# Edge passes of a graph kernel: from 2 gather buffers of 14 columns to 8 of 7, and the edge features and one table fill moved beside the second map scatter

## The chip, the cores and the metric

One NeuronCore of a Trainium2 chip runs the whole program. Its engines are TensorE (PE), VectorE (DVE), ScalarE (ACT), GpSimd (POOL) and the sync engine (SP), each with an instruction stream of its own; semaphores order them. The metric is the device time of one launch in microseconds, the median of three timed runs.

## The reference, cut to what matters

`x` holds 100,000 nodes of 96 float32 features, and `src`, `dst` name the ends of 50,000 edges. Four graph layers follow one another. All of them gather rows of a node table by edge and add them up by node:

```python
# layer 0: ten hops of a weighted sum over edges      layer 1: one GCN convolution
for _ in range(10):
    out = segment_sum(out[dst] * w[:, None], src, n) * 0.9 + h * 0.1
# layer 2: Chebyshev terms of degree 1, 2, 3 with softmax weights, then batch norm
Tx1 = prop(Tx0); Tx2 = 2.0 * prop(Tx1) - Tx0; Tx3 = 2.0 * prop(Tx2) - Tx1   # prop = weighted segment_sum(h[src], dst)
# layer 3: two GINE convolutions; e is computed once per edge
e = relu(edge_weight1 @ W_l0 + b_l0) @ W_l1 + b_l1          # [50000, 96]: the "edge features"
agg = segment_sum(relu(x[src] + e), dst, n)
# after each layer: x = layernorm(x + layer(x))
```

## The kernel before, in words

The edges are sorted twice, by `src` (`sort_src`) and by `dst` (`sort_dst`), so that edges which share a node stand next to each other. An **edge pass** (`edge_pass`) then walks over all edges: 128 partitions times T = 392 columns, one edge in each cell. For each column it gathers 128 table rows by an indirect DMA that POOL issues (L512), multiplies them by the edge weights on ACT (`rows`, L612), and runs a chain along the columns on DVE (L569): `total = previous * joins + rows`, where `joins` is 1 inside a run of equal nodes and 0 at its start. The last edge of a run so holds the sum of its node. Because the next hop only needs the rows at the edges, a hop writes its sums as one row per edge (`Store`), and the table of the next hop has 50,176 rows. The eight hops from the second to the ninth also read a residual row `res` per edge and finish on DVE (L699). Some passes end in `Scatter` instead: POOL also issues one indirect DMA per column which writes the sums to the node table (L745).

The passes stand in this order, with a barrier of all engines between two of them (`Phase.__exit__`): `sort_src`, `sort_dst`, `map_dst` (`scatter_map`, in which POOL alone issues 392 indirect writes), `hop_first`, `hop_second`, three times (`hop_odd`, `hop_even`), `hop_ninth`, `hop_last` (scatters), `gcn` (scatters), `cheb1`, `cheb2`, `cheb3` (scatters, with `MixHops`), `gine1`, `gine2` (scatter), and node passes between them. `MixHops` transposes three 96-feature rows per column on PE, multiplies them by a folded weight, and copies the 292-wide result out on ACT (L887, L894) before POOL scatters it. `FillRows` writes zeros to the tables that are scattered to; in `sort_dst` SP issues 56 writes of 2044 KB for `mixed` among them, while POOL issues 392 map scatters of its own (`MapScatter`) and DVE sorts. `Features` computes the edge features of layer 3 beside `hop_second`, after each batch of it (`beside`).

Within a pass the columns go in **batches** of `GROUP` = 14, and 28 batches in pairs: `raw`, `rows`, `sums`, `res` and `wanted` have two slots each, and `total` has four PSUM banks of four columns (`QUADS`). POOL gathers batch b+1 before it finishes batch b. It may gather into a slot when ACT has weighed the batch that was there two before, by these lines:

```python
            def gather(i, h, first):
                if not first:
                    pool.wait_ge(s["weighed"], i * 8 + h * 4 - 4)
                own.step(nc.gpsimd.tensor_copy(wanted[:, h, :], index[:, bass.ds((i * 2 + h) * GROUP, GROUP)]))
```

SP loads `res` of batch b behind a wait for `copied` of batch b-2 (L680), and behind the store of batch b-1, which waits for the whole of that batch (L683).

## Time and profile before

| | |
|---|---|
| time, median of 3 runs | 19699.26 us (19690.18 to 19725.49) |
| the profiled execution | 19798.93 us, of which the span is 19797.3 us |
| busy: POOL, DVE, ACT, PE | 8959.5, 7463.9, 4583.8, 4154.2 us |
| edge passes | sixteen: ten hops, `gcn`, three of `cheb`, two of `gine` |
| one hop with `Store` and residual, alone | 606 to 622 us |
| `hop_second`, with `Features` beside it | 768.8 us |
| a pass that scatters | 1100 to 1106 us, `cheb3` 1669 us |
| `map_dst` | 511.5 us, POOL alone |

POOL's busy time counts the indirect DMAs themselves (0.95 us each) and not the 0.30 us between two of them, which the profile calls "issue". A pass is read from a window of the trace that holds it alone; its time is the sum of POOL's issue, of what POOL waits for, and of what follows the last gather.

### The profile page before, as it was taken

To read this page: it belongs to the slowest core of one execution; us is meant where nothing else is said; L and a number is where in the kernel's file an instruction comes from. 1 tells how busy PE (TensorE), PEld (TensorE's weight loads), DVE (VectorE), ACT (ScalarE), POOL (GpSimd) and SP (SyncE) were. 2 spreads that over 40 slices of the span, in tenths; PEclk is the share of its full clock that TensorE was granted. 3 is DMA by queue.
4 is the path that set the end of the run, shared out by engine and by line. 5 is a ranking of instruction groups with operands and counts; after the bars stand their busy time and mean duration, and the time that the engine had idled before them with its cause. 6 is when DMAs were issued, how large, how long until landed. Compare 5 with 4: busy or idle time off the path is not lost. (4 is left out here: it accounts for less than half of the span.)

```text
span 19797.3 us, 123940 instructions
## 1 busy us (share of the span) xinstructions
PE 4154.2 (21%) x18516; PEld 3096.2 (16%) x18516; DVE 7463.9 (38%) x23392; ACT 4583.8 (23%) x13127; POOL 8959.5 (45%) x9881
## 2 busy tenths in 40 slices
PE   0000031000000000000036102555555100270078
PEld 0000031000000000000025001444444100150056
DVE  7541233333333332262159321000566741231145
ACT  0001321111111111043135222222111420130045
POOL 0736655566566666725630565444000047407710
PEclk9965555555555555555555555777777555695555
DMA  5901233333333331152135222111333531241144
GB/s 174 378 9 28 70 104 94 93 91 96 93 94 95 90 96 58 48 195 83 30 113 197 76 65 65 63 58 56 127 120 120 174 123 47 85 183 48 47 152 164
DMA packets 691059, 2030.30 MB, mean 103 GB/s; under 512 B 296971, under 2 KB 308950, under 8 KB 669412
## 3 DMA queue, kind: packets, MB, share of 16 engines
q1 hardware_dynamic: 345428, 1385.45, 20.3%
q0 software_dynamic: 329360, 564.80, 10.6%
q10 hardware_dynamic: 16128, 78.68, 1.0%
q14 instruction: 119, 0.97, 0.0%
q8 instruction: 24, 0.39, 0.0%
HBM read 1228.59 MB, written 839.09 MB: 104 GB/s over the span
## 5 line engine op out<-in xcount | busy, mean ns | idle before, releaser
L512 POOL DMA_INDIRECT hop_odd_raw<-hop_table,hop_odd_wanted x1176 | 1116.0, 949 | 416.4 <-issue 388.0
L512 POOL DMA_INDIRECT hop_even_raw<-hop_table,hop_even_wanted x1176 | 1113.5, 947 | 415.6 <-issue 389.6
L745 POOL DMA_INDIRECT sums<-gine_sums,gine_target x784 | 795.2, 1014 | 305.4 <-issue 278.0
L512 POOL DMA_INDIRECT cheb_raw<-cheb_table,cheb_wanted x784 | 744.1, 949 | 272.6 <-issue 263.0
L865 PE MATMUL cheb_mixing<-folded,cheb_hops_turned 96*128 96x292 f32 x2352 | 820.6, 498 | 0.0
L1502 POOL DMA_DIRECT2D mid<-cheb_nodes_rows x56 | 29.9, 533 | 1604.8 <-DVEq L1901 1604.8
L745 POOL DMA_INDIRECT mixed<-cheb_mixed,cheb_target x392 | 385.6, 984 | 759.5 <-ACT cheb_mixed L894 615.8
L569 DVE SCALAR_TENSOR_TENSOR cheb_total<-cheb_ends,cheb_joins,cheb_rows 128x96 f32<-128x96 f32 x84 | 27.3, 325 | 1840.0 <-ACT cheb_rows L612 1758.6
L1723 PE MATMUL cheb_nodes_product<-folded,cheb_nodes_turned_rows 97*128 97x292 f32 x1568 | 547.1, 499 | 693.5 <-DVE cheb_nodes_mixed L1869 590.8
L612 ACT ACTIVATE hop_odd_rows<-hop_odd_raw,hop_odd_weights 128x96 f32<-128x96 f32 x1176 | 321.0, 360 | 1522.1 <-remote 686.5
L612 ACT ACTIVATE hop_even_rows<-hop_even_raw,hop_even_weights 128x96 f32<-128x96 f32 x1176 | 321.0, 360 | 1503.5 <-remote 661.0
L1696 PE MATMUL gine_nodes_hidden<-gine_nodes_turned_rows,gine_nodes_w 96*96 96x512 f32 (+1 forms) x896 | 606.4, 769 | 108.3 <-ACT gine_nodes_turned_rows L1601 108.3
L569 DVE SCALAR_TENSOR_TENSOR hop_odd_total<-hop_odd_total,hop_odd_joins,hop_odd_rows 128x96 f32<-128x96 f32 x1092 | 354.3, 324 | 633.9 <-remote 204.4
L569 DVE SCALAR_TENSOR_TENSOR hop_even_total<-hop_even_total,hop_even_joins,hop_even_rows 128x96 f32<-128x96 f32 x1092 | 354.3, 324 | 619.2 <-issue 183.7
L556 DVE TENSOR_TENSOR gine_raw<-gine_raw,gine_feats 128x1344 f32<-128x1344 f32 x56 | 87.2, 1558 | 1318.6 <-DMA gine_raw<-conv,gine_wanted 524.2
L589 PE MATMUL gine_ends<-gine_tail,dst_carries 128*128 128x96 f32 x4 | 1.5, 475 | 2689.9 <-issue 1614.8
L1715 PE MATMUL gine_nodes_product<-gine_nodes_w,gine_nodes_hidden_rows 96*128 96x96 f32 x3136 | 562.8, 337 | 0.0
L1869 DVE SCALAR_TENSOR_TENSOR cheb_nodes_mixed<-cheb_nodes_mixed,cheb_nodes_factor,cheb_nodes_product 128x292 f32<-128x292 f32 x784 | 384.7, 517 | 457.3 <-PE cheb_nodes_product L1723 417.8
L1715 PEld LDWEIGHTS gine_nodes_product<-gine_nodes_w,gine_nodes_hidden_rows 96*128 96x128 f32 x3136 | 553.9, 258 | 18.3
L865 PEld LDWEIGHTS cheb_mixing<-folded,cheb_hops_turned 96*128 96x128 f32 x2352 | 526.8, 239 | 140.8 <-issue 12.7
L569 DVE SCALAR_TENSOR_TENSOR cheb_total<-cheb_total,cheb_joins,cheb_rows 128x96 f32<-128x96 f32 x1092 | 355.4, 325 | 409.9 <-issue 334.6
L745 POOL DMA_INDIRECT hop_sums<-hop_last_sums,hop_last_target x392 | 384.8, 982 | 198.2 <-issue 135.1
(461 smaller groups left out, 19044.2 us busy)
## 6 DMA issues: line engine op xcount, KB each, us to landing
mixed<-sort_dst_fill SPq DMA_DIRECT2D x56, 2044.0 KB
cheb_nodes_mixed<-mixed SPq DMA_DIRECT2D x56, 2044.0 KB, 9.3
gine_nodes_sums<-sums SPq DMA_DIRECT2D x112, 672.0 KB, 6.2
hop_odd_res<-hop_table SPq DMA_DIRECT2D x84, 672.0 KB
hop_table<-hop_odd_sums SPq DMA_DIRECT2D x84, 672.0 KB
hop_even_res<-hop_table SPq DMA_DIRECT2D x84, 672.0 KB
hop_table<-hop_even_sums SPq DMA_DIRECT2D x84, 672.0 KB
start_x<-x_and_map SPq DMA_DIRECT2D x56, 700.0 KB, 4.4
```

Of the source, the lines that this page charges most:

```text
L512: pool.indirect_dma_start(out=raw_rows[:, h, g, :], out_offset=None, in_=table, in_offset=bass.IndirectOffsetOnAxis(ap=wanted[:, h, g:g + ...
L556: nc.vector.tensor_tensor(raw[:, h, :, :], raw[:, h, :, :], feats[:, h, :, :], ALU.add)\
L569: nc.vector.scalar_tensor_tensor(into, before, joins[:, h, g:g + 1], rows[:, h, g, :], ALU.mult, ALU.add).then_inc(s["chained"], 1)
L589: nc.tensor.matmul(carried, side.carries[:, :], tail[:, :], start=True, stop=True)\
L612: ins = nc.scalar.activation(rows[:, h, g, :], raw[:, h, g, :], ACT.Copy, scale=weights[:, h, g:g + 1])
L745: pool.indirect_dma_start(out=self.out, out_offset=bass.IndirectOffsetOnAxis(ap=self.target[:, h, g:g + 1], axis=0), in_=self.rows(ph, h, ...
L865: ins = nc.tensor.matmul(self.mixing[t % 2][:, 0:MIX], self.turned[:, t % 2, j, :], self.folded[0:C, j + 1, :], start=(j == 0), stop=(j == 2))
L1502: pool.dma_start(node_rows(table, b), flat(tile[:, h, :, :])).then_inc(left[h], 16)
L1696: nc.tensor.matmul(hidden[q % 2][:, 0:n, :].rearrange("c g p -> c (g p)"), d.hidden[0][:, :], turned_rows[0:C, q % 2, 0:n, :].rearrange("c ...
L1715: ins = nc.tensor.matmul(product[q % slots][:, j, 0:d.width], left_side[:, q % 2, j, :], d.weights, start=True, stop=True)
L1723: nc.tensor.matmul(product[t % slots][:, 0, 0:d.width], left_side[:, q % 2, j, :], d.weights, start=True, stop=True).then_inc(s["product"], 1)
L1869: return self.nc.vector.scalar_tensor_tensor(mixed[:, h, g, :], mixed[:, h, g, :], self.factor[:, h, g:g + 1], product[:, 0, 0:MIX], ALU.m ...
```

## The change

The edge passes now go in 56 batches of 7 columns (`EDGE`). The gathered rows have 8 slots (`RAW`), 56 columns in place of 28; `rows`, `sums`, `res`, `joins`, `weights`, `scales` have 4 slots (`WORK`), 28 columns as before. POOL gathers batch b+5 (`AHEAD`) before it finishes or scatters batch b, and copies the indices (`wanted`) of four batches at once. `total` is two pairs of banks, of 4 and 3 columns (`PARTS`). The residual load stands three batches ahead of its use (`Residual.LEAD`), before the store in SP's order. `Features` and the fill of `mixed` leave `hop_second` and `sort_dst` for a phase with the second map scatter (`map_and_features`), with two PSUM tiles for its transposes in place of one. The diff, cut to its core:

```diff
-STEPS = GROUP + 1
+EDGE, RAW, WORK, AHEAD = 7, 8, 4, 5
+PARTS = ((0, 4), (4, 3))
+STEPS = EDGE + 1
...
-def scatter_map(nc, k, name, maps):
+def map_and_features(nc, k, maps, features, fill):
...
         @block.gpsimd
         def _(pool):
+            fill.pool(ph, pool)
             maps.pool(ph, pool)
+        @block.sync
+        def _(sp):
+            features.sync_setup(ph, sp)
+            for b in range(2 * pairs):
+                fill.issue_part(ph, sp, b, 2 * pairs)
+                features.store(ph, sp, b, b % 2)
+            features.sync_end(ph, sp)
+            fill.wait(ph, sp)
...
-        raw_rows = ph.sbuf("raw", [P, 2, GROUP, width])
-        rows = ph.sbuf("rows", [P, 2, GROUP, C])
+        raw_rows = ph.sbuf("raw", [P, RAW, EDGE, width])
+        rows = ph.sbuf("rows", [P, WORK, EDGE, C])
...
             def gather(i, h, first):
                 if not first:
-                    pool.wait_ge(s["weighed"], i * 8 + h * 4 - 4)
-                own.step(nc.gpsimd.tensor_copy(wanted[:, h, :], index[:, bass.ds((i * 2 + h) * GROUP, GROUP)]))
-                own.wait()
+                    pool.wait_ge(s["weighed"], (i * RAW + h - RAW + 1) * len(PARTS))
+                if h % WORK == 0:
+                    if not first:
+                        for n in range(h, h + WORK):
+                            pool.wait_ge(s[f"gathered{n}"], i * (16 * EDGE))
+                    own.step(nc.gpsimd.tensor_copy(wanted[:, h:h + WORK, :].rearrange("p n g -> p (n g)"),
+                                                   index[:, bass.ds((i * RAW + h) * EDGE, WORK * EDGE)]))
+                    own.wait()
                 pool.nop(nofuse=True)
...
-            gather(0, 0, True)
+            for h in range(AHEAD):
+                gather(0, h, True)
             def body(i, first, last):
-                gather(i, 1, first)
-                finish.pool(ph, pool, i, 0, first)
-                if not last:
-                    gather(i + 1, 0, False)
-                finish.pool(ph, pool, i, 1, first)
+                for h in range(RAW):
+                    if h + AHEAD < RAW:
+                        gather(i, h + AHEAD, first)
+                    elif not last:
+                        gather(i + 1, h + AHEAD - RAW, False)
+                    finish.pool(ph, pool, i, h, first)
...
+class Residual:
+    LEAD = WORK - 1
+    def sync(self, ph, sp, i, h, first, last):
+        if last and h + self.LEAD >= RAW:
+            return
+        if not (first and h == 0):
+            sp.wait_ge(ph.sems["copied"], (i * RAW + h) * len(PARTS))
+        if h + self.LEAD < RAW:
+            self.load(ph, sp, i, h + self.LEAD)
+        else:
+            self.load(ph, sp, i + 1, h + self.LEAD - RAW)
...
-        self.turned = ph.psum("f_turned", [C, 4, P])
+        self.turned = [ph.psum(f"f_turned{n}", [C, 4, P]) for n in range(2)]
...
-        fills = FillRows(nc, [(hop_sums, (0.0,)), (sums, (0.0,)), (mixed, (0.0,))]
+        fills = FillRows(nc, [(hop_sums, (0.0,)), (sums, (0.0,))]
...
-        scatter_map(nc, k, "map_dst", maps_dst)
+        map_and_features(nc, k, maps_dst, Features(nc, k, W_l0, b_l0, W_l1, b_l1, feats),
+                         FillRows(nc, [(mixed, (0.0,))]))
...
-        hop("hop_second", Store(nc, k, hop_a, hop_first), hop_first, 2, k.s_second, beside=features)
+        hop("hop_second", Store(nc, k, hop_a, hop_first), hop_first, 2, k.s_second)
```

The first place is POOL in `hop_last`, at the start of the pass; `hop_last_wanted` and `hop_last_target` are the staged indices of gather and scatter. Before:

```order
L508 COPY hop_last_wanted<-i_hop 128x14
L512 DMA hop_last_raw<-hop_table,hop_last_wanted 128x96 x14
L508 COPY hop_last_wanted<-i_hop 128x14
L512 DMA hop_last_raw<-hop_table,hop_last_wanted 128x96 x14
L739 COPY hop_last_target<-src_end 128x14
L745 DMA hop_sums<-hop_last_sums,hop_last_target 100352x96 x14
L508 COPY hop_last_wanted<-i_hop 128x14
```

After:

```order
L546 COPY hop_last_wanted<-i_hop 128x28
L551 DMA hop_last_raw<-hop_table,hop_last_wanted 128x96 x28
L546 COPY hop_last_wanted<-i_hop 128x28
L551 DMA hop_last_raw<-hop_table,hop_last_wanted 128x96 x14
L808 COPY hop_last_target<-src_end 128x7
L814 DMA hop_sums<-hop_last_sums,hop_last_target 100352x96 x7
L551 DMA hop_last_raw<-hop_table,hop_last_wanted 128x96 x7
L808 COPY hop_last_target<-src_end 128x7
L814 DMA hop_sums<-hop_last_sums,hop_last_target 100352x96 x7
L551 DMA hop_last_raw<-hop_table,hop_last_wanted 128x96 x7
```

POOL now stands 42 columns of gathers ahead when it comes to the first scatter (28 before), and from there on 7 gathers and 7 scatters alternate, with one `target` copy for each 7.

The second place is DVE in a hop (`hop_odd`), the first batch of the pass, from its staging copies to its last finish. Before:

```order
L542 COPY hop_odd_joins<-src_joins 128x14
L542 COPY hop_odd_weights<-w_hop 128x14
L542 COPY hop_odd_scales<-s_hop 128x14
L569 SCALAR_TENSOR_TENSOR hop_odd_total<-hop_odd_ends,hop_odd_joins,hop_odd_rows 128x96
L569 SCALAR_TENSOR_TENSOR hop_odd_total<-hop_odd_total,hop_odd_joins,hop_odd_rows 128x96 x7
L699 SCALAR_TENSOR_TENSOR hop_odd_sums<-hop_odd_total,hop_odd_scales,hop_odd_res 128x96 x4
L569 SCALAR_TENSOR_TENSOR hop_odd_total<-hop_odd_total,hop_odd_joins,hop_odd_rows 128x96 x4
L699 SCALAR_TENSOR_TENSOR hop_odd_sums<-hop_odd_total,hop_odd_scales,hop_odd_res 128x96 x4
L569 SCALAR_TENSOR_TENSOR hop_odd_total<-hop_odd_total,hop_odd_joins,hop_odd_rows 128x96 x2
L569 SCALAR_TENSOR_TENSOR hop_odd_ends<-hop_odd_total,hop_odd_joins,hop_odd_rows 128x96
L699 SCALAR_TENSOR_TENSOR hop_odd_sums<-hop_odd_total,hop_odd_scales,hop_odd_res 128x96 x6
```

After:

```order
L583 COPY hop_odd_joins<-src_joins 128x7
L583 COPY hop_odd_weights<-w_hop 128x7
L583 COPY hop_odd_scales<-s_hop 128x7
L611 SCALAR_TENSOR_TENSOR hop_odd_total<-hop_odd_ends,hop_odd_joins,hop_odd_rows 128x96
L611 SCALAR_TENSOR_TENSOR hop_odd_total<-hop_odd_total,hop_odd_joins,hop_odd_rows 128x96 x6
L611 SCALAR_TENSOR_TENSOR hop_odd_ends<-hop_odd_total,hop_odd_joins,hop_odd_rows 128x96
L738 SCALAR_TENSOR_TENSOR hop_odd_sums<-hop_odd_total,hop_odd_scales,hop_odd_res 128x96 x7
L583 COPY hop_odd_joins<-src_joins 128x7
L583 COPY hop_odd_weights<-w_hop 128x7
```

One batch of 14 with the finish of a quad put between the chains of the next quads becomes two batches of 7, each with three staging copies of its own, its chain of 7 in one piece and then its 7 finishes.

SP's order is seen in the diff (`Residual.sync` is called ahead of the wait and the store in `Store.sync`): a residual load now stands ahead of the store of a batch three earlier, where it stood behind the store of the batch before.

## Rows read from the trace of the kernel before

**Rows 1.** The page's costliest groups: `cheb3`'s scatters; busy us, mean ns, idle before, releaser

```profile
L745 POOL DMA_INDIRECT mixed<-cheb_mixed,cheb_target x392 | 385.6, 984 | 759.5 <-ACT cheb_mixed L894 615.8
```

**Rows 2.** Windows: start:end, length, PE PEld DVE ACT POOL busy, PEclk, DMA share, GB/s

```profile
1241.50:1753.00 511.50, 0.00 (x0) 0.00 (x0) 0.00 (x0) 0.00 (x0) 383.51 (x394) 0.50 0.02 1
1768.90:2356.70 587.80, 0.74 (x2) 0.50 (x2) 162.45 (x589) 223.61 (x814) 382.09 (x421) 0.50 0.25 67
2366.40:3135.20 768.80, 292.42 (x1178) 236.80 (x1178) 279.76 (x1037) 185.39 (x506) 378.40 (x421) 0.50 0.32 100
5008.00:5620.00 612.00, 0.74 (x2) 0.50 (x2) 228.88 (x897) 107.58 (x394) 378.33 (x421) 0.50 0.31 95
7481.00:8587.00 1106.00, 0.74 (x2) 0.50 (x2) 235.11 (x897) 107.60 (x394) 770.45 (x841) 0.50 0.17 49
11003.50:11592.00 588.50, 0.74 (x2) 0.50 (x2) 142.73 (x477) 156.47 (x506) 378.42 (x421) 0.50 0.25 67
12194.00:13863.00 1669.00, 974.84 (x3533) 687.70 (x3533) 142.07 (x477) 489.07 (x1292) 771.53 (x841) 0.71 0.18 59
```

**Rows 3.** Groups of POOL instructions, whole span: busy us, mean ns, idle before by releaser

```profile
L508 POOL COPY hop_even_wanted<-i_hop 128x14 int32 (+1 forms) x84 | 17.0, 202 | 245.1 <-ACT hop_even_rows L612 220.1 <-POOLq L86 22.2 <-issue 2.6
...
L508 POOL COPY hop_odd_wanted<-i_hop 128x14 int32 (+1 forms) x84 | 16.8, 200 | 247.1 <-ACT hop_odd_rows L612 217.5 <-POOLq L86 23.1 <-issue 6.3
...
L508 POOL COPY hop_ninth_wanted<-i_hop 128x14 int32 (+1 forms) x28 | 5.6, 199 | 87.4 <-ACT hop_ninth_rows L612 79.4 <-POOLq L86 7.6 <-issue 0.4
...
L508 POOL COPY hop_second_wanted<-i_hop 128x14 int32 (+1 forms) x28 | 5.4, 194 | 222.2 <-ACT hop_second_rows L612 212.3 <-POOLq L86 9.9
```

**Rows 4.** The group of DVE's chain in one hop (5008 to 5620 us)

```profile
L569 DVE SCALAR_TENSOR_TENSOR hop_even_total<-hop_even_total,hop_even_joins,hop_even_rows 128x96 f32<-128x96 f32 x364 | 118.1, 324 | 208.0 <-issue 65.7 <-remote 52.9 <-DMA hop_even_res<-hop_table 45.0
```

**Rows 5.** DVE in that hop in order of time, from 5115 us

```profile
5119.65 0.33 DVE L569 SCALAR_TENSOR_TENSOR hop_even_total<-hop_even_ends,hop_even_joins,hop_even_rows 128x96 f32<-128x96 f32 x1 [6.09 <-issue]
...
5153.91 0.33 DVE L569 SCALAR_TENSOR_TENSOR hop_even_total<-hop_even_ends,hop_even_joins,hop_even_rows 128x96 f32<-128x96 f32 x1 [2.63 <-ACT hop_even_rows L612]
...
5158.24 1.41 DVE L569 SCALAR_TENSOR_TENSOR hop_even_total<-hop_even_total,hop_even_joins,hop_even_rows 128x96 f32<-128x96 f32 x4 [2.92 <-DMA hop_even_res<-hop_table]
...
5164.90 0.17 DVE L542 COPY hop_even_weights<-w_hop 128x14 f32 x1
...
5166.65 0.33 DVE L569 SCALAR_TENSOR_TENSOR hop_even_total<-hop_even_ends,hop_even_joins,hop_even_rows 128x96 f32<-128x96 f32 x1 [1.50 <-issue]
```

**Rows 6.** POOL in the same stretch in order of time

```profile
5156.63 0.19 POOL L508 COPY hop_even_wanted<-i_hop 128x14 int32 x1 [9.53 <-ACT hop_even_rows L612]
5157.61 0.96 POOL L512 DMA_INDIRECT hop_even_raw<-hop_table,hop_even_wanted  x1 [0.79 <-POOL hop_even_wanted L508]
...
5165.13 0.95 POOL L512 DMA_INDIRECT hop_even_raw<-hop_table,hop_even_wanted  x1 [0.30 <-issue]
```

**Rows 7.** The end of that hop, all engines in order of time

```profile
5617.38 1.62 POOL L717 DMA_INDIRECT hop_table<-hop_even_fix,src_fix_row  x1 [17.11 <-DMA hop_table<-hop_even_sums]
```

**Rows 8.** POOL's scatters in `hop_last` (7481 to 8587 us)

```profile
L745 POOL DMA_INDIRECT hop_sums<-hop_last_sums,hop_last_target x392 | 384.8, 982 | 198.2 <-issue 135.1 <-DMA cheb_table<-sort_dst_fill 58.3 <-POOL hop_last_target L739 4.9
```

**Rows 9.** ACT in `cheb3` in order of time

```profile
12826.62 0.41 ACT L894 ACTIVATE cheb_mixed<-cheb_mixing 128x292 f32<-128x292 f32 x1 [9.34 <-DMA gcn_nodes_skip<-x]
...
12841.55 0.41 ACT L894 ACTIVATE cheb_mixed<-cheb_mixing 128x292 f32<-128x292 f32 x1 [0.99 <-PE cheb_mixing L865]
...
12843.36 0.41 ACT L894 ACTIVATE cheb_mixed<-cheb_mixing 128x292 f32<-128x292 f32 x1 [0.99 <-PE cheb_mixing L865]
...
12845.14 3.81 ACT L612 ACTIVATE cheb_rows<-cheb_raw,cheb_weights 128x96 f32<-128x96 f32 x14
```

**Rows 10.** Windows inside `sort_dst`, the columns as in the windows above

```profile
500.00:540.00 40.00, 0.00 (x0) 0.00 (x0) 37.20 (x48) 0.00 (x0) 30.72 (x31) 1.00 1.01 381
540.00:580.00 40.00, 0.00 (x0) 0.00 (x0) 19.14 (x29) 0.00 (x0) 30.65 (x31) 1.00 1.00 378
```

**Rows 11.** ACT's group of the features' quads beside `hop_second`

```profile
L1217 ACT ACTIVATE hop_second_f_hidden<-hop_second_f_turned,hop_second_f_c,hop_second_f_w 96x512 f32<-96x512 f32 x112 | 80.2, 717 | 479.6 <-remote 280.8 <-issue 130.1 <-PE hop_second_f_turned L1231 60.9
```

## What I expect of it

> **What bounds the kernel now.** I first cut the span into its passes with the windows [rows 2]. In every one of them TensorE, VectorE and ScalarE are mostly idle; POOL is busy for 378 of the 612 us of a hop and 770 of the 1106 us of a pass that scatters. POOL's time between two gathers is 0.30 us called "issue" [rows 6], so that one gather costs 0.95 + 0.30 = 1.25 us and 392 of them 490 us. This is the floor of a gathering pass, and the change touches none of it. What a hop takes above it is 612 - 490 = 122 us. Three parts of it can be read: the index copy and the step behind it, 0.19 + 0.79 - 0.30 = 0.68 us, 28 times, 19 us [rows 6]; the end, from the last gather to the write of the carried row, 17 us [rows 7]; and the wait of POOL's index copy for ACT's `rows`, that is for a free `raw` slot: 220.1 us in three even hops, 217.5 in three odd ones, 79.4 in the ninth, 212.3 in the second [rows 3]. That is 73 us a hop, in some eight waits of about 9.5 us [rows 6]. Why ACT is late is seen on DVE, whose chain ACT's slots wait for: DVE needs 12.7 us for one batch (5153.91 to 5166.65) but 34.3 us for another (5119.65 to 5153.91, of it 2.63 us waiting for ACT) [rows 5], where POOL needs 14 x 1.25 + 0.7 = 18.2 us. The mean is near POOL's pace: (31.6 + 2 x 12.7) / 3 = 19.0. Part of it is a wait for `res`, 45.0 us a hop [rows 4], 2.9 us a batch where it occurs [rows 5]. So DVE is late by bursts, and 28 gathered columns are too few to bridge one.
>
> `cheb3` is different: ACT and PE, not POOL, are the bound, since POOL's scatters wait 615.8 us for `mixed` [rows 1] of its 1669 us [rows 2]. The profile's quick columns follow each other in 1.81 us there, while one stands behind a gap of 9.34 us [rows 9]. A batch so costs 1669 / 28 = 59.6 us where POOL issues 14 x (1.25 + 1.28) = 35.4.
>
> **The change, part by part.** The sum is made against the profiled execution (19798.9 us, its span 19797.3); the timed median is 0.5% lower, and I carry the differences over to it unchanged.
>
> *Features leave `hop_second`.* It takes 768.8 us, a like hop 612 [rows 2]: **-157**. What is left behaves as the others.
>
> *56 columns of raw slots, and `res` loaded three batches ahead, in eight hops.* POOL may run 35 columns ahead of ACT rather than 14, which is 21 x 1.25 = 26 us more than now and covers one slow batch (31.6 - 18.2 = 13.4 us late). The wait for `res` should go as well. Against it stands that DVE's mean of 19.0 us is hardly below POOL's 18.2, that DVE now has 84 more short staging copies a hop at 0.17 us (14 us) [rows 5], and that the slow batch may be a consequence of POOL's own steady issue, so that it comes more often when POOL no longer pauses. Bounds: nothing gained, or all 73 us. I take half, 36 us: 8 x 36 = **-288**. The index copy is made 14 times instead of 28, worth at most 14 x 0.68 = 9.5 us a pass; there are 28 more waits of POOL whose price no row shows. I set the two against each other, at nothing.
>
> *`hop_first`, `cheb1`, `cheb2`.* They take 588 us [rows 2], 98 above the floor; less 19 for index copies, 17 for the end and some 10 of set-up, about 50 us are waits. `cheb1` and `cheb2` give back half, 25 each; `hop_first`, which also works on the met rows, 15: **-65**. Bounds 0 and -150.
>
> *Four passes that scatter* (`hop_last`, `gcn`, `gine1`, `gine2`). The floor is 490 + 392 x (0.98 + 0.30) = 992 us [rows 8], the pass takes 1106 [rows 2]. In the 114 us are 56 changes of slot (some 45 us) and the wait of the scatters for a DMA, 58.3 us in `hop_last` [rows 8]. Scattering five batches behind should hide the stalls; I take 33 us a pass as their mean, and 6 us for the shorter last batch. On the other side are 28 more `target` copies at 0.68 us, +18 a pass. Net -21 a pass: **-83**. Bounds +70 and -200.
>
> *`cheb3`.* Halved batches double the fixed part of a batch on ACT (the wait for the chain, the first transpose), some 5 us x 28 = +140 by the gap between its weighing (3.8 us) and a steady column. But POOL's long run of issue, 35 us, becomes shorter ones, and with scatters five batches behind, ACT need not wait for slots; the quick column's pace would make a batch 14 x 1.81 + 8 = 33 us instead of 59.6. If a third of the slow part goes, 28 x 27 / 3 = 250 us are won. I take **-100**, with bounds +150 and -450.
>
> *`map_dst`.* POOL's 511.5 us now cover the features [rows 2]. Beside `hop_second` their 112 quads took ACT 80.2 + 479.6 = 560 us [rows 11], 5.0 us each. At that pace they end 50 us behind POOL. The fill of `mixed` puts 56 x 2.044 = 114 MB under them; at the 380 GB/s of [rows 10] this is 300 us, and so is hidden, but SP issues it ahead of each feature store. Set-up and the last store add some 20. Cover alone would give 0, a pace of 6.8 us a quad (the features beside full queues) 762 us, +250. I take **+110**.
>
> *`sort_dst`.* DVE is busy 37.2 of 40 us at first and 19.1 of 40 later, with the queues full (DMA share 1.00) in both [rows 10]. Some 300 us of full queues leave this phase. If the sort's slow half came from them, up to 160 us would be won; since the share is as high in the quick stretch, most of it has another cause. I take **-50**.
>
> Sum: -157 - 288 - 65 - 83 - 100 + 110 - 50 = -633; 19699 - 633 = 19066, rounded to **19070**.
>
> One rule speaks against the change. [rows 6] shows a gather at 5165.13 us that takes 0.95 us right behind DVE's copy at 5164.90 [rows 5], as long as any other.
> The Trainium skill (page "SBUF — State Buffer", section "SBUF: two separate sides") says that a float32 `tensor_copy` of VectorE inside SBUF locks GpSimd out of the port they share, so that the descriptors of GpSimd's DMAs wait until it ends; the change doubles the number of such copies.
>
> **The rivals.**
>
> *A, partly hidden* (the sum above): 18900 to 19370. Chance 0.55.
>
> *B, the ring hides all of it:* eight hops give 73 rather than 36 us (-296 more), the other gathering passes 65 more; about 18700, and down to 18400 if `cheb3` reaches -450. For it: DVE's quick batch is far below POOL's pace. Against: the mean of 19.0 us. Chance 0.14.
>
> *C, the hops give nothing:* DVE's mean is the bound, whatever the buffers. Then only the moves and the scatters count: -157 - 83 - 65 + 110 - 50 = -245, with `cheb3` at 0: 19450, up to 19620 with the map phase at its worst. Chance 0.13.
>
> *D, slower:* DVE's slow batches become more frequent, because POOL no longer pauses. The point from which it decides: at a share s a batch takes 12.7 + 18.9 s us; a hop stays at 612 / 28 = 21.9 us for s = 0.49, where it is 0.33 now. At s = 0.7 a hop takes 28 x 25.9 = 726 us, 8 x 114 = +912 less the 245 of C: 20370; at 0.6 it is 673 us, +488 - 245, 19940. For it: the slow batch ends with POOL's pause (POOL stops before 5147, DVE is quick from 5153.91 on) [rows 5, 6]. Against: the smaller batches pause DVE's work more evenly. Chance 0.12.
>
> *E, copies hold POOL up:* each of the 84 added copies of a hop keeps a gather for its 0.17 us, 14 us a pass and 16 passes, at most +220: 19290. The row above speaks against it. Chance 0.03. This is what the cited section would make of it.
>
> A last 0.03 is for sums that cancel, near 19700.
>
> **The numbers.** A measurement of this kernel tells 0.2% (39 us) from no change. Faster: A, B, C and E, less a little of C, 0.84; within 0.2% 0.04; slower 0.12. The range holds A, C, E and most of B: 18700 to 19600; A alone 18900 to 19370.
>
> **What would show it.** In the changed profile POOL's wait for ACT's `rows` should fall from 220 to about 110 us for three hops, and a hop take 570 to 580; DVE's wait for `res` should vanish; `hop_second` should be as long as its neighbours; a scattering pass about 1085; `map_dst` 580 to 650; `cheb3` 1500 to 1650. I am wrong if a hop is above 612 (D), or at its floor of about 530 (B), and wrong in a term if the map phase passes 700.

## The result, and the profile after

The changed kernel takes 19939.76 us (19911.26 to 19953.94), the kernel before 19703.25 us beside it: **1.0117 times, interval 1.01 to 1.0135, so 1.2% slower**. The forecast was 19070, with a range to 19600. One thing must be known to read the numbers below: the kernel before took 19700 to 19840 us beside most of the runs, but 17930 us beside the eight of two groups (one of them on the very chip that had given 19724 earlier). I call the first condition A and the second B, and compare only within a group; the prediction and this result stand in A.

Lengths of the phases in the profiled executions, first to last instruction of each, in us (A). `hop_first` is taken with the short step that finds the rows of the next hops:

| | before | changed | forecast of the difference |
|---|---|---|---|
| `sort_dst` | 773.5 | 744.0 | -50 |
| map phase | 511.4 | 797.5 | +110 |
| `hop_first`, `cheb1`, `cheb2` | 1770.6 | 1808.4 | -65 |
| `hop_second` | 768.7 | 629.7 | -157 - 36 |
| the seven hops from third to ninth | 4286.0 | 4408.7 | -252 |
| `hop_last`, `gcn`, `gine1`, `gine2` | 4407.0 | 4390.9 | -83 |
| `cheb3` | 1668.2 | 1496.8 | -100 |
| all to the last instruction | 19788.7 | 19901.0 | -633 |

The rest of the difference is in what stands between phases (+43, of it 19 us from the last instruction of the map phase to the landing of its last writes, so that this phase costs 816 us) and in the node passes behind `gine` (-23). These last are not the change's: in a second trace of the kernel before (k17) they take 600 and 879 us, as in the changed kernel (600 and 883), and not 612 and 894.

The windows of the changed kernel (start:end, length, busy of PE PEld DVE ACT POOL, PEclk, DMA share, GB/s), to be laid beside [rows 2]:

```profile
1212.10:2009.60 797.50, 272.95 (x1176) 241.07 (x1176) 58.30 (x140) 80.75 (x112) 395.56 (x395) 0.50 0.41 166
2038.80:2652.90 614.10, 0.74 (x2) 0.50 (x2) 184.92 (x785) 216.99 (x842) 380.01 (x407) 0.50 0.25 64
2664.90:3294.60 629.70, 0.74 (x2) 0.50 (x2) 249.40 (x1009) 110.64 (x394) 376.04 (x407) 0.50 0.32 92
3941.80:4570.50 628.70, 0.74 (x2) 0.50 (x2) 249.61 (x1009) 110.65 (x394) 376.00 (x407) 0.50 0.32 92
7779.70:8883.40 1103.70, 0.74 (x2) 0.50 (x2) 262.18 (x1009) 110.64 (x394) 778.79 (x855) 0.50 0.18 49
11298.50:11885.00 586.50, 0.74 (x2) 0.50 (x2) 153.94 (x561) 158.67 (x506) 376.09 (x407) 0.50 0.26 67
12503.00:13999.00 1496.00, 997.70 (x3533) 696.91 (x3533) 149.94 (x558) 493.92 (x1292) 779.76 (x854) 0.75 0.21 66
```

POOL's groups over its whole span (busy us, mean ns, idle before by releaser), beside [rows 3, 7]: the wait for a raw slot is no shorter, and the wait at the end of three hops has grown from some 50 (17 in each) to 150 us.

```profile
L551 POOL DMA_INDIRECT hop_odd_raw<-hop_table,hop_odd_wanted x1176 | 1117.0, 950 | 606.6 <-issue 384.8 <-ACT hop_odd_rows L647 218.5 <-POOL hop_odd_wanted L546 3.3
L551 POOL DMA_INDIRECT hop_even_raw<-hop_table,hop_even_wanted x1176 | 1114.1, 947 | 609.9 <-issue 368.7 <-ACT hop_even_rows L647 236.4 <-POOL hop_even_wanted L546 4.9
...
L787 POOL DMA_INDIRECT hop_table<-hop_even_fix,src_fix_row x3 | 4.9, 1624 | 149.7 <-issue 149.7
```

DVE's chain in one hop, beside [rows 4]. The wait for `res` is gone, as forecast, and yet DVE ends later:

```profile
L611 DVE SCALAR_TENSOR_TENSOR hop_even_total<-hop_even_total,hop_even_joins,hop_even_rows 128x96 f32<-128x96 f32 x336 | 109.4, 326 | 100.6 <-issue 43.9 <-DVE hop_even_total L611 43.4 <-remote 3.4
```

DVE in that hop in order of time, beside [rows 5], with the operation's length behind its start:

```profile
4272.06 0.33 DVE L611 SCALAR_TENSOR_TENSOR hop_even_total<-hop_even_total,hop_even_joins,hop_even_rows 128x96 f32<-128x96 f32 x1 [3.86 <-issue]
...
4277.66 1.67 DVE L738 SCALAR_TENSOR_TENSOR hop_even_sums<-hop_even_total,hop_even_scales,hop_even_res 128x96 f32<-128x96 f32 x7 [2.95 <-issue]
...
4281.08 0.33 DVE L611 SCALAR_TENSOR_TENSOR hop_even_total<-hop_even_ends,hop_even_joins,hop_even_rows 128x96 f32<-128x96 f32 x1 [1.53 <-ACT hop_even_rows L647]
4281.44 2.13 DVE L611 SCALAR_TENSOR_TENSOR hop_even_total<-hop_even_total,hop_even_joins,hop_even_rows 128x96 f32<-128x96 f32 x6
...
4287.01 0.33 DVE L611 SCALAR_TENSOR_TENSOR hop_even_total<-hop_even_ends,hop_even_joins,hop_even_rows 128x96 f32<-128x96 f32 x1 [1.42 <-ACT hop_even_rows L647]
...
4303.41 0.33 DVE L611 SCALAR_TENSOR_TENSOR hop_even_total<-hop_even_ends,hop_even_joins,hop_even_rows 128x96 f32<-128x96 f32 x1 [5.99 <-issue]
...
4306.25 0.33 DVE L611 SCALAR_TENSOR_TENSOR hop_even_total<-hop_even_total,hop_even_joins,hop_even_rows 128x96 f32<-128x96 f32 x1 [1.08 <-DVE hop_even_total L611]
```

and POOL beside it:

```profile
4274.27 0.95 POOL L551 DMA_INDIRECT hop_even_raw<-hop_table,hop_even_wanted  x1 [0.31 <-issue]
4282.41 0.94 POOL L551 DMA_INDIRECT hop_even_raw<-hop_table,hop_even_wanted  x1 [7.19 <-ACT hop_even_rows L647]
```

The reader should lay these two on each other. POOL issues its last gather at 4274.27 us and, when it is done, waits 7.19 us. DVE, which stood 3.86 us between two steps of a chain, runs six of them in 2.13 us from 4281.44 on, and a batch in 5.9 us (4281.08 to 4287.01). POOL resumes at 4282.41; DVE goes on quickly for another 15 us, waits 5.99 us for nothing that the profile shows, and from 4303.77 on its steps stand up to 1.4 us apart again. From the third pause on that repeats each 42 us, which is 28 columns.

Where the hop became longer is seen in POOL's rows of one hop, before and after:

```profile
L512 POOL DMA_INDIRECT hop_even_raw<-hop_table,hop_even_wanted x392 | 371.1, 947 | 138.5 <-issue 131.2 <-POOL hop_even_wanted L508 7.1 <-ACT hop_even_rows L612 0.3
L508 POOL COPY hop_even_wanted<-i_hop 128x14 int32 (+1 forms) x28 | 5.6, 201 | 83.7 <-ACT hop_even_rows L612 75.8 <-POOLq L86 7.5 <-issue 0.4
L717 POOL DMA_INDIRECT hop_table<-hop_even_fix,src_fix_row x1 | 1.6, 1622 | 17.1 <-DMA hop_table<-hop_even_sums 17.1
```

```profile
L551 POOL DMA_INDIRECT hop_even_raw<-hop_table,hop_even_wanted x392 | 371.4, 947 | 203.2 <-issue 122.8 <-ACT hop_even_rows L647 78.8 <-POOL hop_even_wanted L546 1.6
L546 POOL COPY hop_even_wanted<-i_hop 128x28 int32 (+1 forms) x14 | 3.0, 218 | 9.5 <-POOLq L88 9.5
L787 POOL DMA_INDIRECT hop_table<-hop_even_fix,src_fix_row x1 | 1.6, 1625 | 49.4 <-issue 49.4
```

The waits for ACT are 76 and 79 us. The index copies, their wait and the issue of the gathers together are 144 us before and 127 after. The end is 17 and 49 us. So the ring saved nothing of the waits, and the end cost 32 us, twice what the rarer copies gave back.

In the map phase the same is seen at large. TensorE makes 42 matmuls in 100 us beside POOL's scatters, and 368 once POOL is done, although the queues are fullest then (DMA share 1.01, 427 GB/s):

```profile
1300.00:1400.00 100.00, 10.46 (x42) 8.61 (x42) 1.55 (x4) 2.88 (x4) 74.17 (x77) 0.50 0.14 50
1850.00:1950.00 100.00, 84.41 (x368) 75.09 (x367) 17.83 (x43) 24.40 (x34) 0.00 (x0) 0.50 1.01 427
```

### The profile page after: what moved, and what is told of

It reads as the page before. It is cut to its first block and busy times, and to the rows that moved or that the text cites. A ratio compares the mean times of both kernels' runs of the same rounds, so it can differ in the third digit from the quotient of the medians.

```text
span 19909.7 us, 128541 instructions
## 1 busy us (share of the span) xinstructions
PE 4129.7 (21%) x18516; PEld 3089.0 (16%) x18516; DVE 7757.5 (39%) x25184; ACT 4602.5 (23%) x13183; POOL 8964.5 (45%) x9797
## 3 DMA queue, kind: packets, MB, share of 16 engines
q0 software_dynamic: 329360, 564.80, 10.6%
## 5 line engine op out<-in xcount | busy, mean ns | idle before, releaser
L695 ACT ACTIVATE gine_sums<-gine_total 128x384 f32<-128x384 f32 x224 | 89.6, 448 | 1862.2 <-DMA sums<-gine_sums,gine_target 1837.1
L814 POOL DMA_INDIRECT sums<-gcn_sums,gcn_target x392 | 387.8, 989 | 185.9 <-issue 133.7
L2062 DVE TENSOR_TENSOR gine_nodes_rows<-gine_nodes_product,gine_nodes_c 128x384 f32<-128x384 f32 x448 | 226.6, 507 | 628.1 <-PE gine_nodes_product L1786 441.9
L1794 PEld LDWEIGHTS cheb_nodes_product<-folded,cheb_nodes_turned_rows 97*128 97x128 f32 x1568 | 340.2, 230 | 839.5 <-DVE cheb_nodes_mixed L1940 705.2
```

The source lines that it names most:

```text
L695: ins = self.nc.scalar.activation(e["sums"][:, w, g0:g0 + n, :], bank[:, 0:n, :], ACT.Copy)
L814: pool.indirect_dma_start(out=self.out, out_offset=bass.IndirectOffsetOnAxis(ap=self.target[:, w, g:g + 1], axis=0), in_=self.rows(ph, w, ...
L1794: nc.tensor.matmul(product[t % slots][:, 0, 0:d.width], left_side[:, q % 2, j, :], d.weights, start=True, stop=True).then_inc(s["product"], 1)
L2062: return self.nc.vector.tensor_tensor(ph.rows[:, h, g0:g0 + n, :], product[:, 0:n, :], self.c1[:, :].unsqueeze(1).to_broadcast([P, n, C]), ...
```

## The experiments

The theory from here on: **while POOL issues an unbroken stream of indirect DMAs, the steps of other engines (their waits, loop counters and semaphores) are slow; a pause of POOL ends this.** The rivals: the halved batches' own instructions, the deeper ring, the fill's full queues, or an instruction stream that is slow by itself.

**k1, k2: the moves.** k1 is the kernel before with `map_and_features` in place of `scatter_map` and `beside=features`, its edge passes untouched. k2 is the changed kernel with this:

```diff
-        map_and_features(nc, k, maps_dst, Features(...), FillRows(nc, [(mixed, (0.0,))]))
+        scatter_map(nc, k, "map_dst", maps_dst)
+        features_alone(nc, k, Features(...), FillRows(nc, [(mixed, (0.0,))]))
```

> The kernel before with only the moves: the features and the fill of the mixed table beside the second map scatter, all edge passes in batches of 14 as before. Theory (POOL's steady stream of indirect DMAs holds the other engines up, so the features crawl under the map scatters): the map phase is again near 800 us (+286), hop_second near 612 us (-157), sort_dst 30 us less, so about +110 us over before, 19810. Rival (the map phase is slow because of something in the new passes' code, or the halved batches carry the loss): the map phase under 600 us and the time below 19650.

> The changed kernel, but the features and the fill run in a phase of their own behind the map scatter, with POOL idle. Theory (POOL's stream is what holds them up): map 511 us, and the features alone at the pace they have in the changed kernel once POOL is done, about 2.7 us a quad, 300 to 330 us, with the fill hidden at over 400 GB/s: sum 820 to 850 us, that is 20 to 50 us more than the 797.5 us of the two together, so the overlap had bought nearly nothing. Rival (the fill's full queues hold the features up): the features alone would take 500 us or more.

k1: 19896.10 against 19724.18, 1.0088 (1.0071 to 1.0105), a loss of 172 us where 110 was expected; its map phase is 797.1 us to the last instruction and 816.2 to the landing of its last writes, as in the changed kernel, so the loss there needs no halved batch. `hop_second` is 617.6 us. k2: 20000.79, 1.0142 (1.0125 to 1.0158). Its map takes 511.4 us, and the features alone 334.7 us, the fill hidden: 846 us, which is 30 more than the 816 of the two together (all to the landing of the last writes). 511 us of cover had so hidden about 30 us of a work of 335. The rival of the full queues falls: beside the fill at 408 GB/s the features take 2.8 us a quad.

**k3, k4: the ring and the batches apart.** k3 keeps batches of 7 and lets POOL run only 28 columns ahead; k4 keeps the 56 columns and goes back to batches of 14, with one set of four banks as in the kernel before.

```diff
 k3
-EDGE, RAW, WORK, AHEAD = 7, 8, 4, 5
+EDGE, RAW, WORK, AHEAD = 7, 8, 4, 3
...
-                if not first:
-                    pool.wait_ge(s["weighed"], (i * RAW + h - RAW + 1) * len(PARTS))
+                if not (first and h < RAW // 2):
+                    pool.wait_ge(s["weighed"], (i * RAW + h - RAW // 2 + 1) * len(PARTS))
 k4
-EDGE, RAW, WORK, AHEAD = 7, 8, 4, 5
-PARTS = ((0, 4), (4, 3))
+EDGE, RAW, WORK, AHEAD = 14, 4, 2, 3
+PARTS = QUADS
```

> The changed kernel, but POOL may gather into a slot only when the batch four before is weighed, as if there were 28 columns of raw slots, and scatters stand 3 batches behind. Theory (DVE's slow stretches bound the hops, the deeper ring only moves the wait from the middle to the end of the pass): a hop stays within 15 us of the changed kernel's 629 us. Rival (the ring hides part of the stalls and the small batches cost more than it gives): a hop of 660 us or more, +300 us in all.

> The changed kernel with batches of 14 columns again (4 raw slots of 14, 2 work slots, four banks), so the same 56 gathered columns, half the batches. Theory (the loss in the hops comes from the halved batches' additional steps on DVE in its slow stretches): a hop takes 600 us or less, and cheb3 goes back towards 1669 us. Rival (the deeper ring itself is the loss, since POOL pauses less and DVE is slow for longer): a hop stays at 625 us or above.

k3: 19762.15, 1.0019 (1.001 to 1.0029), 1.0% below the changed kernel by the two ratios; a hop takes 607 us, outside the 15 us that I allowed. k4: 19998.57, 1.0147 (1.0131 to 1.0164), a hop 622 us, between the 600 of the theory and the 625 of the rival. k1 to k4 ran in one group, so their hops can be laid side by side. The seven from the third to the ninth take on average 630 us with 7 columns and the deep ring (k2), 611 with 7 and the shallow one (k3), 622 with 14 and the deep ring (k4), 617 with 14 and the shallow one (k1). So with either size of batch the deeper ring makes a hop longer, by 19 and by 6 us. POOL's own rows of one hop, k3 first:

```profile
L551 POOL DMA_INDIRECT hop_even_raw<-hop_table,hop_even_wanted x392 | 370.8, 946 | 193.7 <-issue 123.0 <-ACT hop_even_rows L647 69.0 <-POOL hop_even_wanted L546 1.6
...
L787 POOL DMA_INDIRECT hop_table<-hop_even_fix,src_fix_row x1 | 1.6, 1622 | 25.2 <-issue 25.2
```

```profile
L552 POOL DMA_INDIRECT hop_even_raw<-hop_table,hop_even_wanted x392 | 370.9, 946 | 165.1 <-issue 132.2 <-ACT hop_even_rows L648 27.4 <-POOL hop_even_wanted L547 5.5
L547 POOL COPY hop_even_wanted<-i_hop 128x28 int32 (+1 forms) x13 | 2.8, 212 | 42.6 <-ACT hop_even_rows L648 42.5
L788 POOL DMA_INDIRECT hop_table<-hop_even_fix,src_fix_row x1 | 1.6, 1622 | 39.1 <-DMA hop_table<-hop_even_sums 39.1
```

Where the time goes is seen in when DVE is done with the first columns of such a hop: 28 after 64 us in the changed kernel and 65 in k3, but 56 after 152 and 103 us. From the 140th column on both go on at 42 us for each 28, whatever the ring, and some 20 of the 49 us are left at the end. At the start of a pass nothing holds POOL up until the ring is full of rows that ACT has not weighed. In k3 that is after 56 gathers, 72 us into the hop; in the changed kernel only after 98, at 126 us. DVE's first slow steps come 33 us after the first gather, and until POOL's first wait they go on. The halved batches by themselves cost nothing that shows (611 against 617). In `cheb3` they are the gain: 1485 us in k3, 1669 in k4.

**k5, k6, k12: pauses in the hops.** The changed kernel, with this behind the gathers of a batch:

```diff
+                if paused:                      # passes that store; k12: and h % 2
+                    own.step(nc.gpsimd.memset(scratch[:, :], 0.0))
+                    own.wait()
```

`scratch` is 128 x 600 in k5 and k12, 128 x 3000 in k6.

> The changed kernel, in which POOL, in the nine passes that store and the first two of cheb, fills a scratch tile (128 x 600) after every 7 gathers and waits for it: some 0.8 us of pause in each 9.6 us. Theory (DVE's sequencer steps are slow from some 11 us after POOL resumes an unbroken stream of indirect DMAs until it pauses, whatever the reason of the pause): if a short pause is enough to reset it, POOL's waits for ACT (66 us a hop) and most of the 50 us at the end go, and a hop takes 490 + 56 x 1 + 20 = 570 to 590 us. Rival (the slow stretches are a fixed amount of work of DVE or ACT, instruction fetches at the loop's turns for one): the pause only takes the place of waits and a hop stays at 620 to 635 us.

> As the run before, with a scratch tile of 128 x 3000: some 2.8 us of pause in each 11.6 us. Theory: POOL's floor of a hop becomes 490 + 56 x 3 = 658 us; if the slow stretches need an unbroken stream, DVE follows at once and the pass ends some 10 us behind the last gather, 665 to 675 us with no slow steps of DVE left. Rival: slow steps as often as now and a hop of 690 us or more.

> The changed kernel with the pause in the storing passes only after every second batch, 14 gathers. The kernel before had a break of its index copy at each 14 gathers (0.79 us) and was slow all the same; by that the pause is then too rare, and a hop takes 600 us or more with waits of POOL for ACT; if 14 is rare enough, 560 to 570 us.

k5: 19570.52 against 19827.76, **0.9876 (0.986 to 0.9893)**. POOL has 56 fills of 0.62 us more to do in each hop, 35 us and the waits for them, and yet the hop takes 580 us: it does not wait for ACT once, and the end is down to 10.6 us. That is 49 us less than in the first trace of the changed kernel, and some 50 to 60 less than the same hops of k7 below, which ran in the same group with no pause in its hops (633 to 642 us). One hop of k5:

```profile
L553 POOL DMA_INDIRECT hop_even_raw<-hop_table,hop_even_wanted x392 | 371.3, 947 | 154.1 <-issue 130.8 <-POOL hop_even_scratch L558 17.0 <-POOL hop_even_wanted L548 6.3
L558 POOL MEMSET hop_even_scratch<- 128x600 f32 x56 | 34.7, 619 | 0.0
...
L792 POOL DMA_INDIRECT hop_table<-hop_even_fix,src_fix_row x1 | 1.6, 1627 | 10.6 <-issue 10.6
```

k6: 20799.27, 1.0499; a hop is 690 us, the number that the rival gave. But the rival's slow steps are not there: not one step of DVE's chain in that hop is slow. The 690 us are POOL's own, 146.6 us of fills in place of the 34.7 of k5 and the same 154 us between its gathers (I had put the hop at 665 to 675, since I left out what the wait costs). k12 fell into condition B, where it tells nothing of the pause: 18229.01 against 17932.25, hops of 546 us with no wait.

**k7: pauses in the map phase.** One fill of 128 x 1200 after every 7 map scatters.

```diff
+            if ph.name == "map_dst" and t % 7 == 6:
+                nc.gpsimd.memset(self.scratch[:, :], 0.0).then_inc(made, 1)
+                pool.wait_ge(made, 3 + t // 7)
```

> The changed kernel, in which POOL, in the map phase alone, fills a scratch tile (128 x 1200, about 1.3 us) after every 7 map scatters and waits for it. Theory (POOL's unbroken stream holds the features' steps up): with pauses the features run on beside it, and the map phase falls from 797.5 us towards POOL's 511 + 56 x 1.5 = 600 us, below 700 in any case. Rival (each step across engines costs about 10 us as long as POOL scatters at all): the features advance little in the pauses and the phase takes 797.5 + 80 us.

The phase takes 614.6 us instead of 797.5 (615 instead of 817 to the landing of its last writes, k5 being the run without these pauses in the same group), and holds POOL's scatters, all 1176 matmuls of the features and the fill:

```profile
1238.70:1853.30 614.60, 270.09 (x1176) 240.00 (x1176) 58.92 (x140) 80.70 (x112) 449.14 (x451) 0.50 0.58 223
```

The whole is 19900.30, 1.0048 (1.0027 to 1.0069) in place of 1.0117. The rival, by which a step across engines costs 10 us while POOL scatters at all, falls. k5 and k7 are also each other's control: of the same kernel in the same group, each is quick where its pauses are and slow where they are not.

The mean rate of POOL's DMAs does not explain it either: k5 issues the 392 gathers of a hop in 567 us, the changed kernel in 578, waits included. What differs is how long the stream goes on without a break.

**k8: no indirect gathers.** In eight hops POOL issues a plain DMA per column; the gather by index is left out.

> The changed kernel, in which the eight hops with a residual read their rows by a plain DMA for each column in place of the indirect one (still issued by POOL, one per column; the gather by index is left out, the row of the edge's own position is read instead). Theory (it is the indirect DMAs that slow DVE, ACT and SP): DVE and ACT go at their quick pace, 6.1 us a batch, and a hop takes 56 x 6.1 + 20 = 350 to 380 us. Rival (DVE and ACT are slow by their own instruction streams): a hop stays above 500 us.

17796.48 us in one execution; a hop takes 347 us, just below the forecast, with the same instructions on DVE and ACT:

```profile
3054.40:3401.20 346.80, 0.74 (x2) 0.50 (x2) 240.78 (x1009) 110.64 (x394) 213.28 (x407) 0.50 0.59 167
```

DVE's work fits into 347 us; so the rival of an instruction stream slow by itself falls. POOL's stream is shorter here too (0.54 us for each), so this run does not tell whether it is the kind of DMA or its duration; k5 does not either.

The traces hold a direct count of the slow steps, over `hop_second` to `hop_ninth` (from the third hop on in the kernel before, whose second holds the features). A chain step is called slow here when DVE starts it more than 0.8 us after the one before it (most stand 0.36 us apart), a loop-counter instruction when it takes more than 0.5 us itself (most take 0.04); the single slow step of three runs is a remainder:

| | slow chain steps of DVE | slow counter instructions of DVE | of SP |
|---|---|---|---|
| before | 577 of 2156 | 658 of 4043 | 215 of 599 |
| changed | 556 of 2688 | 712 of 3732 | 318 of 1212 |
| k3, shallow ring | 483 of 2688 | 628 of 3732 | 382 of 1212 |
| k7, no pause in the hops | 524 of 2688 | 683 of 3732 | 411 of 1212 |
| k5, short pauses | 45 of 2688 | 123 of 3732 | 273 of 1212 |
| k6, long pauses | 1 of 2688 | 0 of 3732 | 38 of 1212 |
| k8, plain DMAs | 1 of 2688 | 0 of 3732 | 0 of 1212 |
| k13, condition B | 1 of 2688 | 0 of 3732 | 0 of 1212 |

SP's counter instructions touch no tile, and they are slow as well; those of ACT never are (0 of 252 in the changed kernel). In k5 many of SP's are still slow, so its pauses do not end the effect for every engine.

**k9, k10, k11: all pauses, and pauses in the kernel before.** k9: k5's and k7's pauses, and some in `cheb3` and the first map. k11: the same with 128 x 8. k10: the kernel before with

```diff
+                    if isinstance(finish, Store) and g % 7 == 6:
+                        own.step(nc.gpsimd.memset(scratch[:, :], 0.0))
+                        own.wait()
+                        pool.nop(nofuse=True)
```

> The changed kernel with POOL's short pause (a fill of 128 x 600 and a wait for it) after every 7 gathers in the passes that store, around the 7 gathers in cheb3, and after every 7 map scatters in both maps. Theory (an unbroken stream of indirect DMAs slows the others' steps): hops at 580 us, the second map phase near 600 us (-200), sort_dst 100 us shorter since DVE sorts at its pace beside the first map, cheb3 below 1500 us; in all 19570 - 200 - 100 - 50 = about 19220 us, 3% below the kernel before. Rival (DVE in sort_dst and PE in cheb3 are held up by something else): only the map phase gains, 19380 us.

> The kernel before, with its batches of 14 and its 28 columns of raw slots, and the pause after every 7 gathers in the storing passes. Theory (the stream, not the batching or the ring, makes DVE late): a hop takes 490 + 56 x 0.7 + 19 + 17 = 565 to 585 us instead of 609, hop_second well below 768 us, in all 300 to 450 us less than before. Rival (small batches or the ring are needed to profit): a hop stays at 600 us or more.

> The same, the fill being of 128 x 8 only, so that the pause is little more than the wait for it. If the break in the stream itself matters and not its length, the hops take some 20 to 30 us less than with the longer fill, 550 to 560 us, with no waits of POOL for ACT; if a length of 0.7 us is needed, POOL waits for ACT again and a hop stays above 600 us.

All three came in condition B: 18671.18 (1.0413), 18568.69 (1.0354) and 18337.42 (1.0225) against 17932.25. None can be read as meant. They show something else: in B there is nothing to win by a pause, each is pure cost, and `sort_dst`, which no edit of k10 or k12 touches, takes 584 us instead of 773. Phases in which POOL issues no stream, or does so alone, are the same in A and B: `sort_src` takes 432 to 433 us in every trace, `gcn`'s node pass 826 (829 in one), and the second map scatter alone 511.4 in A and 511.3 in k10. So B is no faster chip; it lacks what POOL's stream does to the others.

**k13 to k16: the changed kernel beside the paused ones.** k13 is the changed kernel itself. k14 is k11 once more; k15 is the kernel before with the pauses of k11; k16 is k15 with the moves of k1.

> The changed kernel itself, beside the kernel before on whatever chip it gets. If the steps of the other engines are slow beside POOL's stream there (the kernel before near 19700 us), it is 1.0 to 1.3% slower, as at first. If they are not (the kernel before near 17930 us, as in the last group of runs), the theory says: no hop waits for ACT in either kernel, the map phase hides the features, so -157 us for hop_second less some 40 us for the map phase, -9 us in each of ten hops for the rarer index copies, +95 us in cheb3 for the halved batches: about 17850 us, 0.5% faster.

> The changed kernel with the shortest pauses (a fill of 128 x 8 and a wait) after every 7 gathers in storing passes and cheb3 and every 7 map scatters in both maps. Where the stream slows the others: hops at 553 us without waits for ACT if the break itself is enough, map phase 560 to 600 us, sort_dst 600 to 650 us, in all 19000 us or less; if a length of 0.7 us is needed, hops above 600 us and 19600 us or more. Where it does not: 18340 us, 2.2% above the kernel before.

> The kernel before (batches of 14, 28 columns of slots, features beside hop_second) with the same shortest pauses in the storing passes, cheb3 and both maps. Where the stream slows the others: hops at 490 + 56 x 0.9 + 40 = 565 to 580 us, hop_second near 610 us, cheb3 below 1300 us, in all below 19000 us; then the changed batches were not needed for any of it. Where it does not: about 18300 us, since each pause is pure cost.

> The same with the features and the fill beside the second map scatter, as in the change. Where the stream slows the others: 30 to 80 us below the run before it if the paused map hides the features (600 us for the phase), the fastest version of all. Where it does not: within 50 us of it.

Condition B again. k13: **17886.61 against 17926.61, 0.9977 (0.9968 to 0.9987)**: there the change gains 0.2%, where 0.5% was expected. k14, k15 and k16: 18334.34, 18337.61 and 18416.89, 1.0227, 1.0227 and 1.0257. k16 misses its 50 us beside k15; in its trace one node pass takes 750 us in place of 600, and its four times lie 160 us apart. Windows of k13: the same 100 us of the sort, the map phase, and a hop:

```profile
700.00:800.00 100.00, 11.29 (x48) 9.69 (x48) 84.34 (x100) 4.27 (x8) 74.81 (x75) 1.00 0.02 1
1051.60:1577.40 525.80, 270.36 (x1176) 240.65 (x1176) 57.94 (x140) 80.62 (x112) 386.99 (x395) 0.50 0.68 261
3703.00:4220.00 517.00, 0.74 (x2) 0.50 (x2) 244.45 (x1009) 110.65 (x394) 375.56 (x407) 0.50 0.39 112
```

The first row is to be laid beside the same 100 us of the changed kernel in A:

```profile
700.00:800.00 100.00, 8.47 (x36) 7.27 (x36) 51.21 (x61) 3.25 (x6) 74.79 (x75) 0.65 0.02 1
```

POOL scatters at the same pace in both (75 instructions, DMA share 0.02, so the queues are empty), and DVE is busy for 84.3 us in the one and 51.2 us in the other. In B the map phase hides features and fill in 526 us, and a hop takes 517 us with 1.5 us of wait for ACT:

```profile
L551 POOL DMA_INDIRECT hop_odd_raw<-hop_table,hop_odd_wanted x392 | 370.9, 946 | 128.0 <-issue 115.5 <-POOL hop_odd_wanted L546 10.9 <-ACT hop_odd_rows L647 1.5
```

**k17, k18: a trace of before, and `cheb3` in 14 alone.** k17 is the kernel before. k18 sets the sizes anew around `cheb3`:

```diff
+        EDGE, RAW, WORK, AHEAD, PARTS, BANKS, STEPS = 14, 4, 2, 1, QUADS, 1, 15
         edge_pass(nc, k, "cheb3", by_dst, ...)
+        EDGE, RAW, WORK, AHEAD, PARTS, BANKS, STEPS = small
```

> The kernel before, once more, for a trace. Near 17930 us it should show no slow steps at all: hops of 490 + 19 + 17 = 526 us with no wait of POOL for ACT, sort_dst at 584 us, map 511 us, cheb3 near 1115 us, and hop_second above 600 us only for its features. Against the changed kernel's trace (17873.6 us to its last instruction) the differences are then -9 us in each hop, about -100 us in hop_second, +14 us in the map phase and +100 us in cheb3. Near 19750 us it repeats the trace shown ahead of the prediction, and cheb3 and the hops of the run beside it are to be read against that.

> The changed kernel with cheb3 alone in batches of 14 (4 raw slots, 2 work slots, scatters one batch behind, as before). Where nothing is slowed (the kernel before near 17930 us): cheb3 goes from 1218 back to about 1115 us, and the whole to 17790 us, 0.75% below the kernel before, below both. Where the stream slows the others (near 19750 us): cheb3 goes back to 1675 us, and the whole to 20100 us.

Condition A: k17 19827.30, its phases within 2% of the first trace. k18: 20232.36 against 19837.54, 1.0203 (1.0188 to 1.0218), where 20100 was expected, with `cheb3` at 1672 us. The unedited `cheb3` of the changed kernel takes 1541 us in k7 and 1558 in k8 on that chip, so the halved batches are worth 115 to 130 us there; on the chip of k1 to k4 it is 1669 us (k4) against 1502 (k2). In B I have 1208 us with 7 columns (k13) and 1117 with 14 (k10, whose `cheb3` has no edit), so they cost 91 us. No trace of the kernel before exists in B.

## Why the prediction was wrong, point by point

- **The step that failed is "56 columns of raw slots ... I take half, 36 us: 8 x 36 = -288".** Measured (eight hops, the features' 157 us set apart) it is +141. I had read DVE's slow batches as bursts which a deeper buffer bridges, and had named the doubt that they follow from POOL's steady issue; that doubt is the cause (k5: a hop with pauses is 49 us shorter; k3: with a shallower ring 22). The ring took nothing off POOL's waits (218.5 and 236.4 us in three hops, against 217.5 and 220.1 [rows 3]). It made the first stream of gathers 126 us long instead of 73, with DVE slow through most of it, and the end 50 us instead of 17 [rows 7]. A deeper ring helps when the mean of the slower engine is below POOL's pace, and I took that mean, 19.0 us, from three batches; over a long stretch DVE makes 28 columns in 42 us, 21 for 14, with either ring. Rival C had this (DVE's mean bounds a hop, whatever the buffers), and rival D had the reason. But D's forecast, that slow batches become more frequent because POOL no longer pauses, did not come: POOL waits 79 us in a hop as against 76, and slow chain steps went from 27 to 21 of 100.
- **`map_dst`, forecast +110, measured +286, and +305 to the landing of its last writes.** This is the next largest miss after the ring. I priced the features by their pace beside `hop_second`, 5.0 us a quad [rows 11], and the worst case by "full queues" at +250. The quads took some 25 us beside the scatters (42 matmuls in 100 us are one batch, which has four quads), and the queues were nearly empty (DMA share 0.14). The same cause, and [rows 10] held a trace of it: I put DVE's halved pace down to "another cause" than the fill and didn't ask which. Those rows alone could not have told, since POOL issues as much in the quick stretch as in the slow one (31 scatters in each).
- **`sort_dst`, forecast -50, measured -30 here but -3 to -6 in k1 to k3**, which leave the same fill out. The direction of the 30 us is not shown to be the change's. Some 190 us of its length are gone in B, as is every other slow step; no run in A pauses the first map scatter, so that they come from POOL's stream is inferred.
- **`hop_second` without features, -157:** right. It is as long as its neighbours (629.7 and 628.4 us).
- **`hop_first`, `cheb1`, `cheb2`, forecast -65, measured +38:** as the hops.
- **Scattering passes, forecast -83, measured -16.** In `hop_last` the scatters' idle time beyond issue fell from 63 us [rows 8] to 51, less than the 33 us taken.
- **`cheb3`, forecast -100, measured -171:** right in direction; k3 and k4 show that it needs the small batches and not the ring. Only in A, however.
- **The wait for `res`** vanished as forecast, and gave nothing that shows. No run changes the place of this load alone.
- **The rule of the Trainium skill** (page "SBUF — State Buffer", section "SBUF: two separate sides") would have DVE's copies hold POOL up. The gathers still take 947 to 950 ns, with twice the copies, so this trace does not show it, at 0.16 us a copy. The row set against the rule in the prediction, a gather at 5165.13 us, could not test it: it began as the copies ended. What is seen here goes the other way, from POOL's DMAs to VectorE, and it is not in the reading or writing of tiles: DVE's chain instructions keep their 0.33 us, only the steps between them grow, and SP's counters are slow too.
- **A sum in rival C** does not come out: 19450 with the map phase at its worst, +250 in place of +110, is 19590 and not 19620. Nothing hangs on it.

## What to carry over

When one engine issues small indirect DMAs without a break, look at the pace of the others' smallest steps, before and behind each of its pauses, before any buffer is deepened: a deeper ring can lengthen exactly the stretches that are slow. And take the mean of the slower engine over many batches: if it isn't below the faster one's pace, no ring helps. A pause of some 1.4 us after every 7 gathers gave 1.2% against the kernel before and, by the two ratios, 2.4% against the changed one, by lengthening the engine that seemed to be the bound; and pauses lost 1.6 to 4.1% where the effect was absent, so such a gain must be measured in both conditions. "Hidden beside an engine that only issues DMAs" is not free: price it by a row taken beside the same stream.

## What the hardware showed

- Beside a stream of indirect DMAs, 1.25 us apart, DVE's chain steps stood, in the slow stretches, about 1.4 us apart instead of 0.36 (0.33 us of work in each), and steps between PE and ACT in the map phase some 10 us. The instructions themselves kept their length; counter instructions of DVE and SP took 0.7 us in place of 0.04, those of ACT did not.
- The slowness ended within 4 us of POOL's pause, in the changed kernel as in k3. When it begins differs: the first slow chain step came some 33 us after the first gather of a hop, 21 to 26 us after most of the later pauses, and in `sort_dst` only some 70 us after the first scatter (463 to 536 us). What sets this stays open.
- A pause of 1.4 us in each 10 us (k5: 0.62 us of fill and the wait) was enough to keep DVE ahead of POOL in the hops; single slow steps are still there (45 of 2688, and 22.0 us of idle time ahead of the chain's steps in a hop, against 100.6; 13.7 in condition B). Whether the shortest pauses are, stays open: k11, k14 and k15 came in condition B.
- The effect is absent in condition B, on one chip at a later time and on another; the whole kernel takes 9% less there (17930 against 19724 to 19838 us), and phases without a stream beside other work take the same. What sets the condition was not tried and stays open; nothing in the program does.
- Which path the streams and the steps share stays open as well.
